# Decoder kernel, routed stage: the router's logits computed as eight column-quarter matmuls and turned back by eight more, instead of thirty-two narrow ones

## The reference

```python
xn = xf * rsqrt(mean(xf * xf) + eps)          # xf: 4096 rows of 128
logits = xn @ router_w.T                      # 8 experts
probs = softmax(logits)
topk_p, topk_i = top_k(probs, 2)
rw = topk_p / sum(topk_p)
# each expert takes its first 640 rows (capacity), in the order of the rows
routed = sum over the two chosen experts of rw * (silu(xg @ rg) * (xg @ ru)) @ rd
shared = silu(x @ sg) * (x @ su) @ sd         # all rows, 1024 hidden columns
return shared + routed
```

## Time and profile before

| | |
|---|---|
| time, median of 3 runs | 2008.99 us (2007.59 to 2013.19) |
| profiled execution, own time | 2019.89 us |
| its span, first to last instruction | 2018.1 us |
| mean granted TensorE clock | 0.973 of full speed |
| TensorE matmuls busy | 1878.6 us, 93% of the span |
| TensorE weight loads busy | 1375.5 us, 68% |
| VectorE busy | 1255.0 us, 62% |
| ScalarE busy | 883.4 us, 44% |
| GpSimd busy | 674.6 us, 33% |
| the routed stage's route_and_share | 998.9 to 1188 us of the span |

### The profile page before, as it was taken

How to read it: one execution, slowest core, us unless ns; L and a number is a source line. 1 busy time by engine, 2 the same in 40 slices (tenths; PEclk the granted TensorE clock), 3 DMA queues, 4 the chain that set the end, 5 groups by cost and what they waited for, 6 DMA issues and landing times. The chain is left out here.

```text
span 2018.1 us, 49126 instructions
## 1 busy us (share of the span) xinstructions
PE 1878.6 (93%) x19778; PEld 1375.5 (68%) x19778; DVE 1255.0 (62%) x2879; ACT 883.4 (44%) x1684; POOL 674.6 (33%) x763
## 2 busy tenths in 40 slices
PE   4899999999999999999899999868888999999987
PEld 2566666667888888888666677646666777777743
DVE  5666666637766666666442222236777777777767
ACT  1433333335555555555422223245663444444434
POOL 2111111103333333333205500075522444444446
PEclk8899999999999999999989999989999999999989
DMA  8000000000000000000100012212100000000001
GB/s 291 1 1 0 0 0 0 1 1 1 1 1 0 0 0 0 0 0 1 72 2 26 27 37 93 75 30 54 22 11 3 3 3 2 3 2 3 3 11 32
DMA packets 31366, 40.93 MB, mean 20 GB/s; under 512 B 5225, under 2 KB 25501, under 8 KB 30708
## 3 DMA queue, kind: packets, MB, share of 16 engines
q1 hardware_dynamic: 27124, 31.97, 4.7%
q0 software_dynamic: 4096, 6.83, 1.5%
HBM read 28.30 MB, written 12.06 MB: 20 GB/s over the span
## 5 line engine op out<-in xcount | busy, mean ns | idle before, releaser
L154 POOL TENSOR_TENSOR rstd<-var_eps,minus_half 128x2 f32<-128x2 f32 (+1 forms) x116 | 92.7, 799 | 411.6 <-DVE var_eps L148 409.4
L975 POOL TENSOR_TENSOR xa_probs<-xa_probs,xa_total 128x512 f32<-128x512 f32 x128 | 133.0, 1039 | 196.7 <-DVE xa_total L1041 192.0
L1046 DVE TENSOR_REDUCE xa_top<-ps 128x4 f32<-128x512 f32 x128 | 88.1, 688 | 120.6 <-PE ps L819 119.4
L478 ACT ACTIVATE la_hid<-ps,pack_moe 128x512 f32<-128x512 f32 x128 | 87.7, 687 | 146.4 <-PE ps L310 145.3
L931 ACT ACTIVATE xa_probs<-xa_probs 128x512 f32<-128x512 f32 x128 | 80.7, 630 | 157.5 <-DVE xa_probs L1049 157.5
L808 PEld LDWEIGHTS ps<-xa_kvT,xa_qk_fold 128*128 128x128 f32 x512 | 96.5, 190 | 64.2 <-issue 41.6
L835 PE MATMUL ps<-xa_probsT,xa_kv 128*128 128x512 f32 x256 | 133.4, 603 | 2.1 <-ACT xa_attnT L940 1.8
L819 PE MATMUL ps<-xa_kvT,xa_qT 128*128 128x128 f32 x1024 | 135.2, 275 | 0.0
L2316 PE MATMUL ps<-ba_inT,pack_latent 128*64 128x128 f32 x1920 | 130.6, 279 | 3.9 <-PEq L1697 1.3
L310 PE MATMUL ps<-la_h2T,pack_moe 128*128 128x512 f32 x256 | 132.6, 633 | 1.2 <-ACT la_hid L478 1.2
L808 PE MATMUL ps<-xa_kvT,xa_qk_fold 128*128 128x256 f32 x512 | 130.7, 380 | 0.2 <-ACT xa_kvT L898 0.2
(11 more groups left out here) (338 smaller groups left out, 4173.8 us busy)
## 6 DMA issues: line engine op xcount, KB each, us to landing
expert_weights<-experts_dram SPq DMA_DIRECT2D x8, 768.0 KB, 4.7
slot_rows<-zeros SPq DMA_DIRECT2D x1, 2560.0 KB
expert_rows<-slot_rows SPq DMA_DIRECT2D x8, 320.0 KB, 2.9
result_rows<-ex_result SPq DMA_DIRECT2D x8, 320.0 KB, 2.4
pack_moe<-moe_dram SPq DMA_DIRECT2D x1, 2312.0 KB
pack_latent<-latent_dram SPq DMA_DIRECT2D x1, 2050.0 KB, 19.8
pack_latent<-biased_dram SPq DMA_DIRECT2D x1, 2048.0 KB, 7.5
out_dram<-X SPq DMA_DIRECT2D x8, 256.0 KB, 2.3
```

The source lines that it names most:

```text
L154: pool.tensor_tensor(m.rstd[:, 0:tiles], m.var_eps[:, 0:tiles], m.minus_half[:, 0:tiles], ALU.pow).then_inc(sem.rstd, 1)
L478: act.activation(hid[:, n // F0 % 2, n % F0, :], HIDDEN[n % 2], ACT.Silu, bias=w["b1"][:, n:n + 1]).then_inc(hid_ready, 1)
L975: pool.tensor_tensor(probs[:, u % 4], probs[:, u % 4], over(total[:, u % 4], 2, KEYS), ALU.mult).then_inc(probs_ready, 1)
L1046: dve.tensor_reduce(top[:, s % 4], scores, AX.X, ALU.max).then_inc(top_ready, 1)
```

## The change

The router's weights are padded with zeros to 32 columns. Now they are the stationary operand, and the turned rows move: a matmul takes four tiles (512 columns) through one quarter of the array's columns, and its result lies in one quarter of a bank's partitions. Four such matmuls (`c` from 0 to 3) fill one bank with the transposed logits of sixteen tiles. The first four stand behind unit 1 and write bank 0, the other four stand behind unit 3 and write bank 1. ScalarE copies each bank into a new SBUF tile `logitsT`, behind its SiLU of units 1 and 3. Behind unit 4, where the old `logits` stood, `turn_logits` takes eight 128 x 128 pieces of `logitsT` as the stationary operand and 32 of the identity's columns (4 times 8) as the moving one, and puts the logits into bank 1 in the layout that VectorE reads as before. Two semaphores are added, and one more wait on each of them.

```diff
+        logitsT = sb("logitsT", [P, 2, N])
+        LOGIT_BANKS = (DOWN_BANK, ROUTE_BANK)
...
-                def logits():
-                    pe.wait_ge(last_ready, 1)
-                    for t in range(T):
-                        mm = pe.matmul(bank(ROUTE_BANK)[:, E1 * t:E1 * t + E1], m.turned_rows[:, t, :], w["router"][:],
-                                       start=True, stop=True)
+                def logits(r):
+
+                    if r == 1:
+                        pe.wait_ge(last_ready, 1)
+                    for c in range(4):
+                        at = GT * (4 * r + c)
+                        mm = pe.matmul(bank(LOGIT_BANKS[r])[QUARTER * c:QUARTER * c + QUARTER, :], w["router"][:],
+                                       m.turned_rows[:, at:at + GT, :].rearrange("p t n -> p (t n)"), start=True, stop=True)
+                    mm.then_inc(logitsT_done, 1)
+
+                def turn_logits():
+
+                    pe.wait_ge(logitsT_ready, 2)
+                    for r in range(2):
+                        for t in range(GT):
+                            mm = pe.matmul(bank(ROUTE_BANK)[:, 0:E1 * T].rearrange("p (r c t e) -> p r t c e", r=2, c=4, e=E1)[:, r, t],
+                                           logitsT[:, r, P * t:P * t + P],
+                                           w["ident"].rearrange("p (c q) -> p c q", c=4)[:, :, 0:E1], start=True, stop=True)
                     mm.then_inc(logits_done, 1)
...
                         if g == 0 and f == 2:
                             turn_last()
+                        if g == 0 and f == 1:
+                            logits(0)
+                        if g == 0 and f == 3:
+                            logits(1)
                         if g == 0 and f == 4:
-                            logits()
+                            turn_logits()
...
+                    if n in (1, 3):
+                        act.wait_ge(logitsT_done, (n + 1) // 2)
+                        act.activation(logitsT[:, n // 2, :], bank(LOGIT_BANKS[n // 2]), ACT.Copy).then_inc(logitsT_ready, 1)
...
-    "shared": [("router", (E1,)), ("sg", (FS, P)), ("su", (FS, P)), ("sd", (FS, D))],
+    "shared": [("router", (QUARTER,)), ("sg", (FS, P)), ("su", (FS, P)), ("sd", (FS, D))],
...
-        "router": a["L0_ffn_router_w"].T, "sg": a["L0_ffn_sg"], "su": a["L0_ffn_su"],
+        "router": np.pad(a["L0_ffn_router_w"].T, ((0, 0), (0, QUARTER - E1))), "sg": a["L0_ffn_sg"], "su": a["L0_ffn_su"],
```

More of the change, by code:

```diff
@@ L1144, in route_and_share @@
         rms_ready = sem("rms_ready")
+        logitsT_done = sem("logitsT_done")
+        logitsT_ready = sem("logitsT_ready")
         logits_done = sem("logits_done")
```

## The result

| | before | after |
|---|---|---|
| time, median of 14 runs each | 2010.11 us | 2002.66 us |
| ratio to before | | 0.9965 (95% interval 0.9954 to 0.9977) |
| profiled execution, span | 2018.1 us | 1998.0 us |
| mean granted clock in it | 0.973 | 0.977 |
| first matmul of unit 0 to that of unit 7 | 26.06 us | 16.49 us |

The changed kernel is 0.35% faster, 7.0 us (4.6 to 9.2). The forecast was 8.5 us and a time of 2000.5; measured were 7.0 us and 2002.66. 8.5 us lies inside the interval of the first comparison and at the edge of the second (3.2 to 8.5 us). One of the twelve executions of the changed kernel in the second comparison took 6380 us and is left out of its ratio.

What follows compares the result with a forecast made beforehand. TensorE, busy for 93% of the span, was taken to bound the kernel. Saved 13.74 less 2.54 + 1.78 added gave 9.4 us, less 0.9 made 8.5: 2008.99 - 8.5 = 2000.5 us, range 1996.5 to 2006.5 (own case 1997 to 2003.5).

Steps and rivals of the forecast that it cites:

- The old block: Router's 64 thin passes before unit 5: cost TensorE 13.74 us including slowed units 5 and 6, 6.6 of it the clock's.
- The quarters: Two groups of quarter matmuls on TensorE, quarters side by side: 1.27 us a group, 2.54 together.
- going in and out: Entering and leaving the quarters between full-width units: 0.20 plus 0.21 us for each group.
- Rival A: In a group, passes go in strict program order, five deep instead of two: 1.29 us more each, 2003.1 us; chance 7%.
- Rival B: Quarters don't overlap at 512 columns: 3.85 us a group, 3.4 saved after deduction, 2005.6 us; chance 5%.
- The turn back: Sixteen thin passes behind unit 4 on TensorE, paced by weight loads at full clock: 1.78 us.
- Case C: Clock falls in the turn back all the same: 5.4 us saved, less 0.9, 2004.5 us; chance 10%.
- The copies: ScalarE's two copies of 0.60 us cost nothing; unit 4 hides the second, ready about 0.9 us before the turn.
- The root: GpSimd's root of the mean squares stays hidden at no cost, ready 2.8 us before VectorE wants it.
- The sum: Over the profiled execution: 13.74 us saved, 4.32 added, 9.4 less; 8.5 after a deduction of 0.9.
- a clock that might fall later in the old block: Deduction of 0.9 us (an estimate) from the 9.4 saved, as the clock's fall may differ in other executions.
- Case D: Clock falls in the first group, returns after unit 6: 2 us slower; 12.7 with serial quarters; both forms 4%.

Runs made afterwards that it cites:

- the second comparison: The changed kernel, unchanged, timed again against the kernel before on another chip: ratio 0.9971 (0.9958 to 0.9984), 5.9 us faster.
- before_again: The kernel before, unchanged, profiled a second time: 24.43 us from unit 0 to unit 7, clock falling 4.0 us after the first thin pass.
- thin_spread: Kernel before with its narrow router matmuls in five lots behind units 0 to 4, no quarters: ratio 0.9971, unit 0 to unit 7 in 19.46 us.
- serial_full: Changed kernel with each group as four full-width accumulating matmuls, one after another: ratio 0.9985, unit 0 to unit 7 in 20.97 us.
- turn_twice: Changed kernel with the eight turn-back matmuls done twice, 32 thin passes in a row: unit 0 to unit 7 in 19.97 us.
- late_copy: Changed kernel with ScalarE's second copy behind its SiLU of unit 4 instead of unit 3: unit 0 to unit 7 in 19.63 us.
- one variant: Changed kernel with both groups of quarters and both copies behind unit 3: ratio 0.9945, then 0.9968 when timed again, against the kernel before.

## Why the prediction was right

**The old block.** Its price of 13.74 us was read from one execution and holds in four of five; `before_again` has 12.1. That 6.6 us of it were the clock's is what `thin_spread` gave back, to the tenth: 26.06 - 19.46.

**The quarters.** I took 1.27 us for a group, from a row of 256 columns in 16 parts and the distance in front of it; measured are 1.19. The part that I put at 0.41 for going in and out is 0.33: 0.09 before the first quarter (line 1217's last pass is through at 1003.74, the quarters start at 1003.83), 0.14 until the next unit starts, and 0.10 in that unit. The page "TensorEngine Tiling (Array Packing)" of the Trainium skill, Key Properties, has the change of tiling mode drain the engine; the trace agrees in kind, with 0.33 us for a group, which is small enough for the change to pay in spite of it. Rival A is out: five passes deep would be 2.15 us, and eight passes took 1.00 from the first one's start to the next unit's. The page "TensorE: Matmul & The Clock Gate" of the Trainium skill states under The mechanism that matmuls start and end in strict program order. In this trace that order does not hold a quarter's first pass back behind its neighbour's second: four passes start within 0.02 us at 998.98, before any of the other four, which start at 999.44. Rival B is out by `serial_full`.

**The turn back.** 1.78 us taken, 1.70 + 0.08 measured. Case C, the clock's fall in the turn, didn't come, but `turn_twice` and `late_copy` show how near it was: 1.8 us more of thin passes, or 1.2 us of idle time ahead of them.

**What I put at nothing.** The copies were early by 1.1 us (0.9 taken), and their cover is real. The root was 2.6 us ahead (2.8 taken), unit 7 started 16.5 us after unit 0, and the waits for VectorE stayed at 3.9 us.

**The sum.** 9.42 us were forecast for a profiled execution, and the stretch has 9.57 for the first pair and 9.25 for the means. What reaches the end is less than the forecast's 8.5 us, 7.0 and 5.9, though neither interval leaves 8.5 clearly outside. I had taken off 0.9 for a clock that might fall later in the old block. That was mostly wrong, since the fall is early in four of five: the old stretch is 0.32 us shorter in the mean than in the first profile (25.74 against 26.06). That 8.5 came as near as it did is in part luck: the 0.9 stood in for a loss that the prediction put at nothing, about 2 us in the experts' stage. It had said that all engines stand to each other as before from unit 7 on. The traces bear that out to the end of the routed stage, and speak against it behind it; the cause is open, as said above. Case D, the slower one, has nothing for it: the clock stayed up through both groups. Its sum has a slip that changes no chance: going in and out of two groups is 0.4 us in its first form and 0.8 in its second, and with 0.8 the first form is 2.5 us slower instead of 2.

## What to carry to other kernels

A long run of matmuls with few moving columns had two prices here: its weight loads, and the clock that it took down, which the dense work behind it then paid too. Spreading the run among dense matmuls gave the second back with no other change, and it was two thirds of the gain in the stretch (6.6 of 9.57 us); look for it before rewriting the arithmetic. When a narrow product must stay, letting the wide operand move through quarters of the array can be worth its way back: here it gave 3.0 us more. And judge such a change by the stretch that it touches: in the changed kernel that repeats to 0.01 us, while two comparisons of whole runs gave 7.0 and 5.9 us, and one variant 11 and then 6.5.

## What the runs showed of the hardware

- Idle time and thin passes together took the clock down: 1.2 us of wait followed by 1.8 us of thin passes in `late_copy` (one execution). The 1.8 us alone did not in three profiles of the changed kernel, nor did 1.6 us of wait ahead of passes of 128 moving columns.
- The clock does not come back at once with dense work: in the kernel before it stayed at 0.50 for 4.8 us of dense units (1019.07 to 1023.9).
- Four quarters with 512 moving columns each take 1.00 us from the first one's start to the next full-width matmul, where the same columns one after another take 3.43.
- Executions of one kernel on different chips differ by up to 8.5 us in the causal stage alone (243.9 and 252.5 us for the kernel before), more than the whole change is worth in time.
